# Two attention layers, a quantized feed-forward and an expert layer on one core: load order, a second queue for the query copies, the epsilon on VectorE, an earlier expert product, and new engine orders

## What is computed

```python
x = x + _L0_xattn_ref(_layernorm(x), ctx_768, ...)   # 16 heads of 8, 77 keys, biases
x = x + _L0_ffn_ref(_layernorm(x), ...)              # fake-quantized, silu(gate) * up, 352 wide
x = x + _L1_xattn_ref(_layernorm(x), ctx_768, mask, ...)
x = x + _L1_ffn_ref(_layernorm(x), ...)              # 8 experts of 256, gelu, all summed, one gate factor
# attention: softmax(q k^T / sqrt(8)) v, then Wo
# fake quantization: clip(round(v / scale), -128, 127) * scale with scale from max|v| over the whole tensor
```

## Time and profile before

| | |
|---|---|
| median of 3 runs | 358.16 us |
| the profiled execution | 357.13 us, span on the core 355.3 us |
| PE busy | 290.0 us (82%) |
| DVE busy | 259.4 us (73%) |
| ACT busy | 154.3 us (43%) |
| POOL busy | 105.0 us (30%) |
| mean granted PE clock | 0.897 of full |

### The profile page before, as it was taken

The page is one execution under the profiler, slowest core; times in us unless marked ns, Lnnn a source line. Parts: engine busy times, 40 slices in busy tenths (PEclk is TensorE's granted clock), DMA queues, the critical chain, the costliest instruction groups (busy, mean ns, idle before and its releaser), DMA issues.

```text
span 355.3 us, 4665 instructions
## 1 busy us (share of the span) xinstructions
PE 290.0 (82%) x1368; PEld 180.3 (51%) x1368; DVE 259.4 (73%) x717; ACT 154.3 (43%) x252; POOL 105.0 (30%) x119
## 2 busy tenths in 40 slices
PE   8594887788886363449778989989999999999995
PEld 3262433444444221223455354624678888888883
DVE  4868368878384489883877377772799998898883
ACT  1110255455663175241025355647734554554541
POOL 5785602001001499021108001010136611603400
PEclk9986599999999857696756599999999999999998
DMA  8558131300005900302223121000000000000000
GB/s 153 168 153 202 45 74 22 83 17 2 8 0 95 241 3 0 118 0 63 64 53 72 27 52 44 9 0 9 2 2 0 0 31 1 0 31 0 1 30 30
DMA packets 12298, 16.92 MB, mean 48 GB/s; under 512 B 3672, under 2 KB 6712, under 8 KB 12265
## 3 DMA queue, kind: packets, MB, share of 16 engines
q1 hardware_dynamic: 10018, 11.75, 14.0%
q0 software_dynamic: 1856, 4.27, 4.6%
q10 hardware_dynamic: 400, 0.61, 0.7%
HBM read 4.90 MB, written 1.05 MB: 17 GB/s over the span
## 4 chain that ended last, share of the span: by engine, by line
PE 45%; DVE 16%; ACT 4%; issue 3%; POOL 1%; DMA 1%; SPq 0%; DVEq 0%; POOLq 0%; ACTq 0%
PE ps_acc L1118 4%; PE ps_acc L1117 4%; PE ps_acc L1116 4%; PE ps_tok L986 4%; PE ps_key L995 3%; PE ps_acc L1144 3%; DVE mx L676 3%; PE ps_key L1103 2%; PE ps_key L902 2%; DVE axb L888 2%; PE ps_key L1104 2%; PE ps_key L1105 2%; PE ps_tok L1103 2%; PE ps_tok L1105 2%; PE ps_tok L1104 2%
## 5 line engine op out<-in xcount | busy, mean ns | idle before, releaser
L676 DVE TENSOR_REDUCE mx<-ps_tok 128x4 f32<-128x312 f32 x128 | 57.2, 476 | 23.4 <-PE ps_tok L986 22.1
L467 ACT ACTIVATE big<-ps_key 117x512 f32<-117x512 f32 (+1 forms) x96 | 53.7, 594 | 42.7 <-PE ps_key L995 41.8
L986 PE MATMUL ps_tok<-kst,qst 97*128 97x312 f32 x128 | 50.7, 433 | 17.2 <-DVE mx L676 11.6
L350 POOL TENSOR_SCALAR veps<-mv 128x4 f32<-128x4 f32 x16 | 4.3, 271 | 157.3 <-DVE mv L584 157.2
L986 PEld LDWEIGHTS ps_tok<-kst,qst 97*128 97x128 f32 x128 | 27.5, 219 | 42.3 <-DVE mx L676 20.7
L825 DVE TENSOR_TENSOR qst<-big,qst 128x512 fp32r<-128x512 f32 x64 | 44.3, 692 | 2.2
L995 PE MATMUL ps_key<-qst,kst 105*117 105x512 f32 (+1 forms) x96 | 41.8, 469 | 4.6 <-ACT big L467 3.7
L902 PE MATMUL ps_key<-spin 128*128 128x512 bf16 x109 | 35.0, 469 | 1.4 <-DVE spin L862 1.4
L527 ACT ACTIVATE big<-ps_tok,b 128x512 f32<-128x512 f32 x32 | 21.9, 689 | 22.7 <-PE ps_tok L1105 21.8
L527 ACT ACTIVATE big<-ps_key,b 128x512 f32<-128x512 f32 x32 | 22.1, 689 | 22.5 <-PE ps_key L1105 20.9
L823 DVE CAST qst<-big 128x512 fp32r<-128x512 f32 x64 | 27.0, 422 | 5.4 <-ACT big L527 5.2
(11 more groups left out here) (199 smaller groups left out, 538.6 us busy)
## 6 DMA issues: line engine op xcount, KB each, us to landing
qst<-qhi SPq DMA_DIRECT2D x64, 64.0 KB, 2.0
qst<-qlo SPq DMA_DIRECT2D x32, 64.0 KB, 2.0
w1f<-in_w POOLq DMA_DIRECT2D x2, 1024.0 KB, 7.7
kst<-rbuf SPq DMA_DIRECT2D x12, 156.0 KB, 7.3
kst<-rbuf POOLq DMA_DIRECT2D x12, 117.0 KB, 6.1
x<-in_x SPq DMA_DIRECT2D x4, 256.0 KB, 9.2
out<-xn SPq DMA_DIRECT2D x4, 256.0 KB, 2.0
qst<-mthl SPq DMA_DIRECT2D x32, 16.0 KB
```

Of the source, the lines that this page charges most:

```text
L467: act.activation(p[0:w, j, :], key[n % 2][0:w, :], ACT.Exp, scale=SCALE).then_inc(q["p_ready"], 1)
L676: nc.vector.tensor_reduce(mx[:, u % 2, t, g, 0, :], tok[n % 2][:, 0:KG].rearrange("p (h j) -> p h j", h=HG), AX.X, ALU.max).then_inc(q["to ...
L986: mm(tok[n % 2][:, 0:KG], qst[0:MASKROW + 1, s, g, 128 * t:128 * t + 128], kst[0:MASKROW + 1, b, g, :], start=True, stop=True).then_inc(q[ ...
```

## The change

1. `late_loads` is called behind SP's `max` job of unit 0 and no longer behind its `q` job.
2. In batch 0 of both layers (units 0 and 4) the second high copy of each group is issued by ACT, right behind its own `qhi` eviction: four transfers on ACT's queue, eight on SP's.
3. The addition of epsilon moves from POOL to DVE, behind a wait of DVE for its own statistics. The semaphore `eps_self` is gone.
4. Expert step 0 on PE no longer waits for `p_ready`; step 2 does. On ACT step 0 waits for all `pv` but two, step 4 for all but one.
5. New strings in `ORDER` and new numbers of unneeded matmuls.

```diff
@@ ORDER["PE"][0]: one line of the table
-        "spin0/0 spin0/1 xt/0 spin0/2 spin0/3 vr0/0 q/0 spin0/4 tok/0/0-1 vr0/1 tok/0/2-3 spin0/5 vr0/2 tok/0/4 xt/1 vr0/3 tok/0/5-6 q/1 tok/0/7 "
+        "xt/0 spin0/0 vr0/0 spin0/1 q/0 spin0/2 spin0/3 spin0/4 tok/0/0-1 spin0/5 tok/0/2 vr0/1 spin0/6 tok/0/3 vr0/2 xt/1 tok/0/4 vr0/3 tok/0/5-6 "
...
-        SPIN = ((3, 4, 4, 0, 8, 3, 4, 2), (8, 4, 6, 0, 12, 0, 0, 0, 1, 1))
-        IDLE = ((8, 7, 2, 5), (5, 0, 2, 5))
+        SPIN = ((2, 0, 0, 0, 19, 11, 0, 5), (1, 2, 7, 0, 2, 7, 3, 1, 2, 2))
+        IDLE = ((9, 7, 0, 4), (2, 0, 4, 5))
...
                             move(qst[0:32, s, g, :], qhi[r, u % 2, :], stack_q[u % 2][g])
-                            move(qst[64:96, s, g, :], qhi[r, u % 2, :], stack_q[u % 2][g])
+                            if b > 0:
+                                move(qst[64:96, s, g, :], qhi[r, u % 2, :], stack_q[u % 2][g])
...
-                        if u == 0:
-                            late_loads()
                     if job == "max":
                         sp.wait_ge(q["mt_split"], u + 1)
                         for g in range(G):
                             move(qst[MHI:KROWS, u % 3, g, :], mthl[8 * g:8 * g + 8, u % 2, :], stack_m[u % 2][g])
+                        if u == 0:
+                            late_loads()
...
-                done(nc.gpsimd.tensor_scalar(veps[:, b, :], mv[:, b, :, 1], LN_EPS, None, ALU.add), "eps_self")
                 done(nc.gpsimd.tensor_tensor(rstd[:, b, :], veps[:, b, :], mhalf[:, 0:NT], ALU.pow), "rstd_ready")
...
                         act.activation(qhi[:, u % 2, :], m1[:, :], ACT.Identity, bias=bq[:, L:L + 1]).then_inc(q["q_hi"], 1)
+                        if b == 0:
+                            act.wait_ge(q["q_hi"], u + 1)
+                            if u >= 3:
+                                act.wait_ge(q["key_put"], 12 * (u - 2))
+                            for g in range(G):
+                                act.dma_start(qst[64:96, u % 3, g, :].bitcast(F32), qhi[32 * g:32 * g + 32, u % 2, :].bitcast(F32)
+                                              ).then_inc(stack_q[u % 2][g], 16)
...
-                    if n == 0:
-                        act.wait_ge(q["pv_put"], 6 * B)
+                    if n in (0, G):
+                        act.wait_ge(q["pv_put"], 6 * B - 2 + n // G)
...
-                ins.then_inc(q["var_ready"], 1)
+                link(ins)
+                nc.vector.tensor_scalar(veps[:, b, :], mv[:, b, :, 1], LN_EPS, None, ALU.add).then_inc(q["var_ready"], 1)
...
                         pe.wait_ge(q["tok_maxed"], 32 * B)
+                    if n == 2:
                         pe.wait_ge(q["p_ready"], 24 * B)
```

More of the change, by code:

```diff
@@ L236, in build @@
             "const_set spin_set extra_ready v_cleared kt_put k_first k_split vr_put v_set xb_set "
-            "var_ready eps_self rstd_ready xn_ready xt_put xt_copied q_put q_hi q_lo "
+            "var_ready rstd_ready xn_ready xt_put xt_copied q_put q_hi q_lo "
             "tok_put tok_maxed mt_put mx_doubled mt_hi mt_split key_put p_ready pv_put o_copied on_put o_normed ot_put ot_copied "
```

## The result

The changed kernel takes 340.29 us (median of 6 runs, 337.61 to 341.06), the kernel before beside it 357.11. The ratio is 0.959, 95% interval [0.952, 0.967]: faster by 17 us where 5.4 were forecast, and outside the range of 347.0 to 359.5. The profiled execution took 339.97 us, 337.0 of them span, against 357.13 and 355.3.

What follows compares the result with a forecast made beforehand. PE bounds the expert phase; ahead of it a chain across engines at half clock sets the time. Terms 1.9 + 0.8 + 1.9 + 0.6 + 0.2 = 5.4 us off 357.1, plus 1.0 for the median: 352.7 us, range 347 to 359.5.

Steps and rivals of the forecast that it cites:

- The transposes themselves: Unit 0's maxima: DVE loses a 1.10 us normalization ahead of them, PE gains two tok matmuls (0.89); half a microsecond sooner.
- term of 1.9: Start of layer 0: half a microsecond at unit 0's transposes plus 1.4 to its first key; ends -1.7 and 4.5.
- The mechanism priced at 0.8: End of layer 0: key ahead of nt/2's transposes, so the last product follows them directly; gain 0.8, from 0 to 0.9.
- Copies on ACT's queue: Units 0 and 4: four copy issues leave SP, hidden by DVE's widening of the keys; 0, from 0 to 0.6.
- Unit 2's copies: Behind the late loads they still land in time (2.0 us landing), 0; a 7.0 us landing stalls PE 4.3.
- So the maxima end 2.2 us sooner: Start of layer 1, unit 4: down/2 moved into DVE's waits ahead of the maxima; part of a gain of 1.9.
- Rival A: PE's clock also rises at the first keys of units 0 and 4, 5.2 us more, 347.5 us; chance 0.15.
- The other moves of the tables: Remaining reorderings in the order tables: priced at 0, from -1 to 1 us.
- First expert product: Expert phase: one product (0.79 us) moves into a PE wait of 0.76; gain 0.6, from 0 to 0.8.
- Epsilon: Addition on DVE instead of POOL saves about 0.1 per norm on the path; gain 0.2, from -1.0 to 0.6.
- Rival C: Bulk transfers delay copies PE needs at units 1 and 2 (1.7 loss, 4.3 stall), 360.6 us; chance 0.11.
- Rival B: First keys come earlier but later waits and slower clock spells absorb the lead, 357 to 358.5 us; chance 0.18.

Runs made afterwards that it cites:

- t0: Kernel before with the change's layer-0 order and unneeded-matmul numbers, late loads still ahead of unit 1's copies: 353.41 us, ratio 0.990.
- p1: Kernel before with only the late loads moved behind unit 0's maxima: 358.81 us, ratio 1.006.
- no1: Changed kernel with the late loads back ahead of unit 1's copies: 342.29 us, ratio 0.961.
- st2: Changed kernel with three DVE jobs (statistics of batches 2 and 3, normalization of batch 2) back between unit 0's maxima: 343.40 us, ratio 0.966.
- clk0: Changed kernel without any unneeded matmuls in layer 0: 342.64 us, ratio 0.966.
- no2: Changed kernel with all twelve query copies of units 0 and 4 back on SP's queue: 339.94 us, ratio 0.957.
- dn2: Changed kernel with DVE's down/2 back behind the first two maxima of unit 4: 341.11 us, ratio 0.962.
- clk1: Changed kernel without any unneeded matmuls in layer 1: 346.72 us, ratio 0.976.
- aft2: The changed kernel itself, measured again in a later call: 342.10 us, ratio 0.965 to the kernel before.
- t1s: Kernel before with the change's layer-1 order and relaxed expert waits, but the old unneeded-matmul numbers: median 349.94 us, ratio 0.977.
- bon: Kernel before with 19 more unneeded matmuls in PE's waits between unit 4's maxima: 356.52 us, ratio 1.006.
- aon1: Changed kernel with 12 more unneeded matmuls in PE's waits at the end of unit 4's maxima: 339.66 us, ratio 0.957.
- no4: Changed kernel with expert step 0 back behind the last products and the old waits: 342.01 us, ratio 0.965.

## Why the prediction was wrong

- **"The transposes themselves: ... I take half a microsecond"** is the first step that failed. They come 4.3 us sooner. I counted the 1.10 us normalization and set two matmuls against it, and did not count the two statistics (1.24 us each with their aggregate), the waits of 1.15 us that PE had beside them, or that all of it was moved into an earlier wait. Its mechanism, the order and the loads together, is the one that t0, p1, no1 and st2 show at this place. From the transposes to the first key 1.4 was forecast and 1.0 came in the two profiles, 0.1 in the means. The maxima were ready at 32.6, but SP sent them at 34.92, behind unit 1's copies, and PE waited 1.67 us for them. So the term of 1.9 measured 5.3. But the step also took for granted that this lead reaches the end, and no1 shows that it needn't: its first key comes at 40.93, 3.9 us later than in the changed kernel, and its time can't be told from it.
- **What layer 0 gave behind its first key** is the larger error there. The sum had 0.8 for it, all at the end of the layer, and priced the other moves at 0. It was 3.4 us in the means of 5 and 7 profiles, and by luck 0.8 in the two that are shown. Of this, 3.1 lie between unit 3's transposes and the first global maximum: 33.4 to 35.9 us with the old tables, 31.4 with the new in six of seven profiles, 32.3 in the one shown. The mechanism priced at 0.8, the product right behind `nt/2`, is right: the last product comes 0.59 us behind these transposes and not 1.57. But the transposes of `nt/2` also come 0.9 us sooner behind unit 3's (16.77 and 17.63), and clk0, the same tables without unneeded matmuls, took 34.7 us from unit 3's transposes, as the old ones did. So this part needs the unneeded matmuls of layer 0, which the sum gave nothing.
- **Copies on ACT's queue, 0:** right (no2). **Unit 2's copies, 0:** right in the shown profile only, which has no wait for them at tok/2/0. Nine of the 12 profiles with the new order and the moved loads have one, of 0.7 to 1.5 us, for a copy that PE could use 3.0 to 3.3 us after its issue. That is above the 2.0 that was taken and far from the 7.0 of the other end. The loads took 4.8 us of SP's time and not 7.0, so the copies were issued at 43.20 and not 46.5. The formula that the prediction quotes from the Trainium skill (DMA: Bandwidth & Descriptors, Anatomy of one DMA) stands there for transfers that GpSimd issues, and these are SP's.
- **"So the maxima end 2.2 us sooner"** is the second step of the sum that failed; it was 5.3 in the two profiles and 4.1 in the means. down/2 is 1.75 of it (dn2), so that mechanism was right. A part of what was missed is the clock: PE at half clock was slow in unit 4's first norm, queries and maxima (q 2.08 us then and 1.12 now), and clk1 puts the 31.4 us at 33.7 when the clock is low throughout. I knew the row and used it only for the lower end. t0 had the same slow q (2.07 us) and took 35.0, so 1.7 of the 5.3 belong to the one profile.
- **Rival A's half.** Unit 4's keys, which the sum had at 0, gave 4.4 us in the two profiled executions. Most of that is which outcome the clock took in the one and in the other (t0 11.1, aft2 14.3, before 15.1). It had 0.15, for a reason that holds only in part: t1s keeps the old numbers and has the short stretch too. The row at 30 us, which the prediction calls in agreement with the Trainium skill (TensorE: Matmul & The Clock Gate, Part 1: The HAM clock gate), shows half clock beside a PE that was busy for 6.75 of 10 us. That is the lower level and not what ends it; the 0.92 for 0.57 in bon is the row that agrees.
- **"The other moves of the tables I price at 0, from -1 to 1"**: unit 6 to unit 7 alone gave 1.5, seen as 15.0 to 15.4 in all profiles with the new order but one (15.8 in aon1), and 16.6 to 18.0 with the old one. Such a stretch can be measured well in a trace, and the bound of 1 had nothing behind it.
- **First expert product, 0.6:** 0.5 by the stretch, in every profile; no4 doesn't single it out. **Epsilon, 0.2:** no effect can be told.
- **Rival C** (bulk loads delay what PE has at its head) acts in these runs, 8.13 and 5.53 us of wait where the loads stand ahead of unit 1's copies (t0, no1). It couldn't act there in the changed kernel, since the change takes the loads away from that place. At unit 2 it acted with 0.7 to 1.5 us in most profiles, in place of the 4.3 that it was priced at.
- **Rival B** (the lead is taken back) is right for the loads: of the 5.7 us that they are worth at unit 0's transposes nothing that can be told reaches the end. It is wrong for the whole kernel, since the orders gain elsewhere.

What stays open: the split of the gain between order and clock is known to some 4 us only, since no kernel was seen to hold the clock through unit 4's keys in every profile. The 1.5 us of unit 7 has a candidate but no test, and for some 1 us of unit 4's maxima there is neither.

## What to carry to other kernels

Price a moved job by everything that stood in its place: the engine's other jobs between two dependent ones, and the waits that both engines had around them. Ask of two edits whether one opens the way for the other; here the order of layer 0 gained nothing at the transposes without the moved loads, nor these without the order. Follow a lead to the end before you put it into a sum: 5.7 us at the first transposes were lost on the way. Where a chain runs at the lower clock, give the sum a term for it, and compare stretches between the same events over several profiles, since one profile has one outcome of the clock.
